# A third expert routed through the slots, with the FFN's second half unrolled

## The chip, the cores and the metric

The kernel runs on one core of one Trainium2 chip. The core's engines run at the same time, each through a program of its own, and wait for one another by semaphores: PE (TensorE) multiplies, DVE (VectorE) and ACT (ScalarE) work elementwise, POOL (GpSimd) does too and issues the indirect DMAs, SP issues the other DMAs. The metric is the device time of one execution in microseconds (us), the median of three runs.

## The reference

4096 rows (2 x 2048) of 256 floats pass through an FFN, causal attention and the same FFN again, each added to what came in. The FFN, shortened:

```python
xln = _ln(x, ln1_w, ln1_b)
att_out = jax.nn.sigmoid(xln @ Wr) * (xln @ Wv) @ Wo
rwkv_state = xln @ Ws
x = x + att_out
h = _ln(x, ln2_w, ln2_b)
...
bids = confidences * capital_shares * difficulty + affinity
winners = jnp.argmax(bids, axis=-1)
...
hr = jnp.square(jax.nn.relu(jnp.einsum('nc,ech->enh', flat_h, K_rwkv)))
out_rwkv = jnp.einsum('enh,ehc->enc', hr, V_rwkv)
out_trans = flat_h @ W1 * jax.nn.sigmoid(flat_state @ W2) @ W3
all_out = jnp.concatenate([out_rwkv, out_trans[None]], axis=0)
...
final = jnp.einsum('ne,enc->nc', onehot, all_out) * scale
return x + final.reshape(B, T, C)
```

Each row needs only the winner's output. Experts 0 and 1 (rwkv) have a hidden width of 1024; the third (trans) has three 256x256 products and a gate made of the first normalized rows z (`flat_state @ W2`).

## The kernel before

A product in float32 is three matmuls (`passes`, L409 to L413): both operands are split in a high and a low part, hi·hi, hi·lo and lo·hi. ACT makes the high parts, DVE or POOL the low ones.

**Part A** of an FFN (`ffn_a_*`) goes through 8 groups (NG) of 512 rows, 4 tiles of 128. For a group PE transposes z (`transpose_z`), projects it (`U`: r, v and the state's gate, 36 matmuls of 512 columns), multiplies by Wo (24 of 256), turns the second normalized rows h (`T2`), computes the bids, then `W1` (12 of 512) and `W3` (24 of 256): the third expert is computed for every row. DVE makes the statistics (`row_stats` L921/927, `stats2` L974/978), the low parts (L949, L960), gv (L954), x2 (L967), the residual (L984), the gates and counts of the routing (`gates` L1000 to L1014, `win` L1018 to L1035, `rank` L1041), the third expert's gate (`g2` L1049) and its sum into the rows (`w3` L1058). POOL turns variances into factors (`rs1` L843 to L848, `rs2` L857 to L860), makes g2's low part (L864) and sends each group's rows, 514 floats long, to their places in a table in DRAM (`scatter` L885, 4 indirect DMAs a group; the last two groups by halves, L875). Rows of expert 0 fill the table from one end, rows of expert 1 from the other. Work on group g is spread over the iterations k = g to g+2; `rows` and `posi` have two buffers, so `residual(g)` waits for the scatter of group g-2 (semaphore `scat`).

**Part B** (`ffn_b_*`) takes the table in 17 slots: 16 of 256 rows and a last one of 128. A slot belongs to expert 0 or 1, read from a table of flags; both K and V stand twice in the program, under `If`/`Else`. PE transposes a slot's h (`sT` L1259), multiplies by K in four quarters (48 matmuls), and V (48 matmuls) one slot behind. ACT makes relu (L1367) and the high part (L1375), DVE the square (L1418), POOL the square's low part (`hr_lo`, L1478), DVE the output rows (`orow` L1425/L1427), which POOL sends back by two indirect DMAs (`send` L1485). Slots 3 to 14 are a loop over two slots on each engine. SP loads a slot's h and rest from the table (L1194, L1199; first use L1206). The table is filled with pad rows ahead of it by SP (`fill`, 16 or 17 DMAs of 514 KB, ahead of each FFN's scatters).

Order on the engines is written by hand, in the loops over k at the end of the functions.

## Times and profile before

| | us |
|---|---|
| runs | 1048.12, 1055.21, 1056.48 |
| median | 1055.21 |
| profiled execution | 1054.12 |
| its span (first to last instruction) | 1052.3 |

| stage | from | to | long |
|---|---|---|---|
| FFN 1, part A (from the first projection) | 12.98 | 207.13 | 194.2 |
| FFN 1, part B, then attention | 207.13 | 661.22 | 454.1 |
| FFN 2, part A | 661.22 | 844.41 | 183.2 |
| FFN 2, part B | 844.41 | 1052.3 | 207.9 |

A stage of part B begins with the first matmul by K of slot 0. Busy shares over the span are PE 93%, DVE 65%, ACT 54% and POOL 47%; the granted TensorE clock has a mean of 0.976. A line of the timeline is: start us, duration us, engine, line, operation, what it writes and reads, how many, and in brackets the idle time of the engine ahead of it with what ended it. In the windows "(x208)" counts instructions.

### The profile page before, as it was taken

What the parts mean: (1) busy time and instruction counts of PE and PEld (TensorE: products, weight loads), DVE (VectorE), ACT (ScalarE), POOL (GpSimd) and SP (SyncE); (2) the same over time, 40 slices, a digit from 0 to 9 for tenths busy, and PEclk for the clock granted to TensorE, in tenths of its full rate; (3) what the DMA queues carried; (4) which work ended last, traced back from release to release, by engine and by line L of the source; (5) the groups of instructions that cost most, each with busy time, mean ns of one, the idle gap of its engine ahead of it and who ended that gap; (6) DMA issues with size and microseconds to landing.
All of it is one profiled execution on the core that took longest, in us unless ns stands there. A gap on an engine that the chain in (4) does not pass through costs nothing.

```text
span 1052.3 us, 21504 instructions
## 1 busy us (share of the span) xinstructions
PE 975.9 (93%) x6960; PEld 900.9 (86%) x6961; DVE 687.6 (65%) x1762; ACT 565.1 (54%) x1201; POOL 490.0 (47%) x539
## 2 busy tenths in 40 slices
...
GB/s 285 178 112 61 81 161 126 96 72 62 61 57 60 60 70 35 111 31 44 65 105 110 51 121 160 101 47 95 62 41 81 81 77 78 60 60 60 61 70 32
DMA packets 51237, 88.96 MB, mean 85 GB/s; under 512 B 5806, under 2 KB 43568, under 8 KB 49968
## 3 DMA queue, kind: packets, MB, share of 16 engines
...
q14 instruction: 34, 0.28, 0.1%
HBM read 58.39 MB, written 47.06 MB: 100 GB/s over the span
## 4 chain that ended last, share of the span: by engine, by line
PE 65%; DVE 18%; ACT 5%; issue 4%; POOL 3%; DMA 1%; another core or an unknown queue 0%; DVEq 0%; POOLq 0%; ACTq 0%; SPq 0%
PE banks4to L412 31%; PE bank L412 24%; PE banks4to L1733 3%; DVE out_rows L1058 2%; DVE pT_lo L2023 2%; DVE gT_lo L960 1%; PE bank L1745 1%; PE bank L508 1%; ACT p L1893 1%; PE bank L1259 1%; DVE chunk_max L2013 1%; POOL attn_x L2121 1%; DVE zT_lo L949 1%; PE bank L498 1%; DVE r_gate L954 1%
## 5 line engine op out<-in xcount | busy, mean ns | idle before, releaser
L1418 DVE TENSOR_TENSOR relu_squared<-relu 128x512 f32<-128x512 f32 (+1 forms) x136 | 151.6, 1124 | 108.1 <-ACT relu L1367 48.6
L1478 POOL TENSOR_TENSOR hr_lo<-relu_squared,hr_hi 128x512 fp32r<-128x512 f32 (+1 forms) x136 | 183.8, 1364 | 58.3 <-DVE relu_squared L1418 55.8
L1367 ACT ACTIVATE relu<-bank,slot_k_bias 128x256 f32<-128x256 f32 (+1 forms) x204 | 83.7, 461 | 177.7 <-PE bank L412 164.0
L412 PE MATMUL banks4to<-v_hi,hr_hi 128*128 128x256 f32 x528 | 151.5, 287 | 2.5 <-DVE slot_out L1427 2.5
L412 PE MATMUL banks4to<-v_lo,hr_hi 128*128 128x256 f32 x528 | 148.7, 282 | 0.0
L412 PE MATMUL banks4to<-v_hi,hr_lo 128*128 128x256 f32 x528 | 148.6, 281 | 0.0
L412 PE MATMUL bank<-shT_hi,k_hi 128*128 128x256 f32 (+1 forms) x408 | 118.1, 289 | 11.1 <-DVE shT_lo L1408 5.8
L412 PE MATMUL bank<-shT_hi,k_lo 128*128 128x256 f32 (+1 forms) x408 | 115.9, 284 | 0.0
L412 PE MATMUL bank<-shT_lo,k_hi 128*128 128x256 f32 (+1 forms) x408 | 115.8, 284 | 0.0
L885 POOL DMA_INDIRECT routed_rows<-out_rows,row_index x48 | 48.1, 1002 | 117.0 <-DVE row_index L1041 106.0
L412 PEld LDWEIGHTS banks4to<-v_hi,hr_hi 128*128 128x128 f32 x528 | 99.5, 188 | 2.9 <-issue 2.9
L412 PEld LDWEIGHTS banks4to<-v_hi,hr_lo 128*128 128x128 f32 x528 | 99.6, 189 | 0.0
L412 PEld LDWEIGHTS banks4to<-v_lo,hr_hi 128*128 128x128 f32 x528 | 99.5, 188 | 0.0
L1375 ACT ACTIVATE hr_hi<-relu 128x512 fp32r<-128x512 f32 (+1 forms) x136 | 84.3, 620 | 16.6 <-ACT relu L1367 8.2
L412 PEld LDWEIGHTS bank<-shT_hi,k_hi 128*128 128x128 f32 x408 | 78.2, 192 | 14.7 <-issue 14.5
L412 PEld LDWEIGHTS bank<-shT_hi,k_lo 128*128 128x128 f32 x408 | 78.3, 192 | 0.0
L412 PEld LDWEIGHTS bank<-shT_lo,k_hi 128*128 128x128 f32 x408 | 78.2, 192 | 0.0
L1893 ACT ACTIVATE p<-banks4to,minus_row_max 128x512 f32<-128x512 f32 (+2 forms) x80 | 49.8, 628 | 35.6 <-DVE minus_row_max L2016 27.8
L1902 ACT CAST pT_hi<-bank 128x512 fp32r<-128x512 f32 (+1 forms) x72 | 39.2, 565 | 41.4 <-PE bank L1745 40.8
L2023 DVE TENSOR_TENSOR pT_lo<-bank,pT_hi 128x512 fp32r<-128x512 f32 (+1 forms) x72 | 47.0, 658 | 19.4 <-ACT pT_hi L1902 18.9
L1485 POOL DMA_INDIRECT x_after_ffn<-slot_out,token_index x33 | 34.3, 1040 | 52.9 <-DVE slot_out L1427 45.5
L1485 POOL DMA_INDIRECT out_x<-slot_out,token_index x33 | 32.6, 989 | 53.7 <-DVE slot_out L1427 46.3
...
## 6 DMA issues: line engine op xcount, KB each, us to landing
...
```

The costliest lines, as they stand in the source:

```text
L412: mm = pe.matmul(outv, w(pw), m(pm), start=(n_first and k == 0), stop=(n_last and k == 2))
L885: pool.indirect_dma_start(routed, bass.IndirectOffsetOnAxis(b.posi[g % 2][:, t:t + 1].bitcast(U32), 0), b.rows[g % 2][:, t, :], None).then ...
L1058: last = dve.scalar_tensor_tensor(rows[:, t, RES], b.bank(6 + t // 2)[:, (t % 2) * C:(t % 2 + 1) * C], b.gt[p][:, t:t + 1], rows[:, t, RES ...
L1367: last = act.activation(b.r[q % 2][:, h % 2, 0:width(j)], b.bank(1 + q)[:, (h % 2) * SLOT:(h % 2) * SLOT + width(j)], ACT.Relu, bias=b.kbs ...
L1375: act.activation(b.hr[p][0][:, 2 * q:2 * q + 2, 0:width(j)], b.r[q % 2][:, :, 0:width(j)], ACT.Square).then_inc(f["hrhi"], 1)
L1418: dve.tensor_tensor(b.sq[q % 2][:, :, 0:width(j)], r, r, ALU.mult).then_inc(f["sq"], 1)
L1478: pool.tensor_tensor(b.hr[p][1][:, 2 * q:2 * q + 2, 0:n], b.sq[q % 2][:, :, 0:n], b.hr[p][0][:, 2 * q:2 * q + 2, 0:n].bitcast(F32), ALU.su ...
L1485: pool.indirect_dma_start(dst, bass.IndirectOffsetOnAxis(b.idx[p][:, t:t + 1].bitcast(U32), 0), b.o[p][:, t, :], None, bounds_check=N - 1, ...
L1733: mm = pe.matmul(out[:, at:at + n], b.kq[pw][:, q, 0, t * P:(t + 1) * P], part, start=(k == 0 and i == 0 and not last), stop=(k == 2), ski ...
L1893: act.activation(b.p[s % 2][t][:, c * KEYS:c * KEYS + w], bank(("S", s, t, c))[:, 0:w], ACT.Exp, bias=b.nbias[:, s % 2, t:t + 1], accum_ou ...
L1902: act.copy(b.pT[m % 2][0][:, 0:w], b.bank(m % 2)[:, 0:w]).then_inc(a["pthi"], 1)
L2023: dve.tensor_tensor(b.pT[m % 2][1][:, 0:w], b.bank(m % 2)[:, 0:w], b.pT[m % 2][0][:, 0:w].bitcast(F32), ALU.subtract).then_inc(a["ptlo"], 1)
```

## The change

Rows of all three experts are routed. The table has three regions of 33 tiles and a pad tile; a row has 770 floats, since it carries z too. Pad rows are written only behind the end of each region (`pads`, 3 indirect DMAs); `fill` is gone. In part A, the state's gate, W1 and W3 are gone from the dense work, with DVE's g2 and w3, POOL's g2 low part and ACT's sig_s and g2_hi; POOL copies z to the rows (`rowz`). The third expert's first products are brought to K's form: for it, a slot's first half is h by W1 and its second half z by the product of Ws and W2, gated by DVE (`gated`), and its W3 stands behind the V of the others. A slot's K of the first half is still chosen by `If`/`Else`; that of the second half is loaded for each slot from DRAM by POOL (`k_in`, 2 DMAs of 512 KB, software queue) in `b.kx`, and V is addressed by a register. There are 18 slots, 16 pairs and 2 singles, unrolled. The first six (EARLY_SLOTS) are made of rows of the first four groups (`early_slots`, in iteration 5 of part A), the others by `late_slots`; the routing of groups 6 and 7 now runs between the first slots of part B.

The core of the diff, on DVE (part A's loop), POOL and PE:

```diff
-ROW = 2 * C + 2
+REGION = N // P + 1
+PAD_TILE = EXPERTS * REGION
+ROWS = (PAD_TILE + 1) * P
+IDX, RES, GATE, Z1 = C, slice(C + 1, 2 * C + 1), 2 * C + 1, 2 * C + 2
+ROW = 3 * C + 2
...
     for k in range(NG):
+        if k:
+            r.residual(k - 1)
+        gv(k, 0)
+        if k >= 2:
+            r.bid_sum(k - 2)
+            r.gates(k - 2)
+        gv(k, 1)
...
+        g_lo(k)
+        if k >= 2:
+            r.win(k - 2)
+            r.rank(k - 2)
+        if k + 1 < NG:
+            z_lo(k + 1)
+        if k:
+            r.h_lo(k - 1)
...
+        if k + 2 < NG:
+            row_stats(dve, b, f, n, k + 2)
+        x2(k)
+        stats2(k)
...
+    def rowz(g):
...
+        if g >= 2:
+            pool.wait_ge(f["scat"][g % 2], 16 * GT * (g // 2))
+        for t in range(GT):
+            last = pool.tensor_scalar(b.rows[g % 2][:, t, Z1:ROW], b.x[g % X_BUFS][:, t], w[:, 4, t:t + 1], w[:, 6, t:t + 1],
+                                      ALU.mult, ALU.add)
...
     for k in range(NG):
-        if 0 <= k - 1:
-            rs2(k - 1)
-        if 0 <= k - 2:
-            lo(k - 2, 0, b.sg[k % 2], b.g2T, f["g2hi"], f["g2lo"])
-            lo(k - 2, 1, b.sg[k % 2], b.g2T, f["g2hi"], f["g2lo"])
+        if k:
+            rowz(k - 1)
         if k + 2 < NG:
             rs1(k + 2)
-        if k == NG - 1:
+        if k == NG - 2:
             pool.drain()
-        if 0 <= k - 2:
+        if k >= 2:
             scatter(k - 2)
+        rs2(k)
...
+    def k_in(j):
...
+        e = pool.value_load(b.slots[0:1, 3, j:j + 1], min_val=0, max_val=EXPERTS - 1)
+        if j >= 2:
+            pool.wait_ge(f["Ks"], 4 * (j - 1))
+        for p in range(2):
+            pool.dma_start(b.kx[j % 2][p][:].rearrange("p c n -> p (c n)"), b.firsts[bass.ds(e * P, P), p]
+                           ).then_inc(f["k_in"][j % 2], 16)
...
+    for j in range(3, NSLOT):
+        for n in range(4):
+            hrlo(j, n)
+        pool.drain()
+        if j + 2 < NSLOT:
+            k_in(j + 2)
+        send(j - 1)
...
+        row = pe.value_load(b.slots[0:1, 2, j:j + 1], min_val=0, max_val=CC + HC)
+        for t in range(tiles_of(j)):
+            for n, h in enumerate((4, 5, 6, 7, 2, 3, 0, 1)):
+                mm = passes(pe, b.bank(0)[:, t * C:(t + 1) * C], lambda p: b.hr[j % 2][p][:, h, t * P:(t + 1) * P],
+                            lambda p: b.V[p][:, bass.ds(row + h, 1)], n == 0, n == HC - 1)
```

POOL's program before, around its scatters of part A; the line numbers in these rows are those of each kernel's own file, a name behind "waits" is the semaphore (`f_st1`: the statistics of the next group's rows, by DVE's row_stats; `f_posr`: the rows' places, by DVE's rank):

```order
L864 TENSOR_TENSOR g2T_lo<-s_gate_62,g2T_hi 128x512 [waits f_g2hi] x2
L843 TENSOR_SCALAR rsqrt_work<-mean_var 128x4 [waits f_z,f_y,f_st1]
L844 TENSOR_SCALAR rsqrt_work<-mean_var 128x4
L845 TENSOR_SCALAR rsqrt_work<-mean_var 128x4
L846 TENSOR_TENSOR rsqrt_work<-rsqrt_work,minus_half 128x8 [waits f_plink]
L848 TENSOR_TENSOR rsqrt_work<-rsqrt_work 128x4 [waits f_plink]
L848 TENSOR_TENSOR rsqrt_work<-rsqrt_work 128x4
L885 DMA routed_rows<-out_rows_64,row_index 4224x514 [waits f_posr,f_rdone,f0_pad]
L885 DMA routed_rows<-out_rows_64,row_index 4224x514 x3
```

The same place in the changed kernel:

```order
L1485 TENSOR_SCALAR out_rows_71<-x_rows_58,rsqrt_work 128x256 x4
L1457 TENSOR_SCALAR rsqrt_work<-mean_var 128x4 [waits f_z,f_y,f_st1]
L1458 TENSOR_SCALAR rsqrt_work<-mean_var 128x4
L1459 TENSOR_SCALAR rsqrt_work<-mean_var 128x4
L1460 TENSOR_TENSOR rsqrt_work<-rsqrt_work,minus_half 128x8 [waits f_plink]
L1462 TENSOR_TENSOR rsqrt_work<-rsqrt_work 128x4 [waits f_plink]
L1462 TENSOR_TENSOR rsqrt_work<-rsqrt_work 128x4
L1495 DMA routed_rows<-out_rows_70,row_index 12800x770 [waits f_rowz,f_posr,f_res,f_z2]
L1495 DMA routed_rows<-out_rows_70,row_index 12800x770 x3
L1471 TENSOR_SCALAR rsqrt_work<-mean_var 128x4 [waits f_z2,f_st2]
```

The place of the scatter behind rs1 is the same; rowz (L1485) stands where the low parts of g2 stood, and rs2 has moved behind the scatter.

DVE's program before, from the residual of iteration 3 (group 2) to the statistics of group 5, in two pieces. First the residual, which waits for the scatter of group 0 (`f0_scattered0`), and what follows it:

```order
L984 SCALAR_TENSOR_TENSOR out_rows_64<-y_rows_59,x_rows_51 128x4x256 [waits f0_scattered0]
L1041 TENSOR_TENSOR row_index<-gate_work,banks4to 128x4 [waits f_pref]
L949 TENSOR_TENSOR hT_lo<-bank,hT_hi 128x512 [waits f_hhi] x2
L967 TENSOR_TENSOR y_rows_60<-banks4to,y_rows_60 128x512 [waits f_Wo,f_y]
L967 TENSOR_TENSOR y_rows_60<-banks4to,y_rows_60 128x512 [waits f_Wo]
```

Then, four rows of `stats2` later, the end of iteration 3 and the start of the next (L921/L927 are row_stats; their end sets `f_st1`, for which POOL's rs1 waits):

```order
L1049 SCALAR_TENSOR_TENSOR s_gate_62<-bank,bias_cols,s_gate_62 128x512 [waits f_W]
L1049 SCALAR_TENSOR_TENSOR s_gate_62<-banks4to,bias_cols,s_gate_62 128x512 [waits f_W]
L990 COPY bid_rows<-banks4to 128x32 [waits f_bidT]
L991 TENSOR_TENSOR bid_rows<-banks4to,bid_rows 128x32 [waits f_link]
L921 BN_STATS bn_parts<-x_rows_51 128x6 [waits f_x_in2,f_st1]
L921 BN_STATS bn_parts<-x_rows_51 128x6 x3
L927 BN_AGGR mean_var<-bn_parts 128x2 [waits f_rs1,f_link]
L927 BN_AGGR mean_var<-bn_parts 128x2 x3
L954 SCALAR_TENSOR_TENSOR r_gate<-bank,bias_cols,r_gate 128x512 [waits f_U,f_sigr]
```

The changed kernel, at the end of iteration 4 and the start of iteration 5:

```order
L1076 TENSOR_TENSOR hT_lo<-bank,hT_hi 128x512 [waits f_hhi] x2
L1045 BN_STATS bn_parts<-x_rows_59 128x6 [waits f_x_in2,f_st1]
L1045 BN_STATS bn_parts<-x_rows_59 128x6 x3
L1051 BN_AGGR mean_var<-bn_parts 128x2 [waits f_rs1,f_link]
L1051 BN_AGGR mean_var<-bn_parts 128x2 x3
L1274 TENSOR_TENSOR y_rows_67<-banks4to,y_rows_67 128x512 [waits f_Wo,f_y]
L1274 TENSOR_TENSOR y_rows_67<-banks4to,y_rows_67 128x512 [waits f_Wo]
L1281 BN_STATS bn_parts<-y_rows_67 128x6 [waits f_x2,f_rs2]
L1281 BN_STATS bn_parts<-y_rows_67 128x6 x3
L1285 BN_AGGR mean_var<-bn_parts 128x2 [waits f_link]
L1285 BN_AGGR mean_var<-bn_parts 128x2 x3
L1082 SCALAR_TENSOR_TENSOR out_rows_70<-y_rows_67,x_rows_57 128x4x256 [waits f0_scattered0]
```

The statistics of the next group (L1045/1051) have moved from the head of an iteration to its end, and the residual (L1082) from its end to the head of the next one, so that x2 and stats2 stand between the two.

## Rows read from the trace of the kernel before

**Rows 1.** Windows: part B of FFN 1, part A of FFN 2; busy us by engine.

```profile
300.00:325.00 25.00, 24.64 (x208) 24.45 (x207) 13.40 (x20) 12.71 (x29) 15.86 (x13) 1.00 0.22 63
...
700.00:725.00 25.00, 24.67 (x154) 21.67 (x154) 21.89 (x77) 17.54 (x34) 10.90 (x16) 1.00 0.18 64
```

**Rows 2.** Timeline of PE: the first matmuls of the four stages.

```profile
12.98 0.77 PE L412 MATMUL bank<-zT_hi,w_hi 128*128 128x512 f32 x1 [0.75 <-DVE zT_lo L949]
...
207.13 0.38 PE L412 MATMUL bank<-shT_hi,k_hi 128*128 128x256 f32 x1 [1.17 <-DVE shT_lo L1408]
...
661.22 0.47 PE L412 MATMUL bank<-zT_hi,w_hi 128*128 128x512 f32 x1 [0.47 <-DVE zT_lo L935]
661.53 0.39 PE L412 MATMUL bank<-zT_hi,w_lo 128*128 128x512 f32 x1
661.76 0.39 PE L412 MATMUL bank<-zT_lo,w_hi 128*128 128x512 f32 x1
...
844.41 0.38 PE L412 MATMUL bank<-shT_hi,k_hi 128*128 128x256 f32 x1 [1.09 <-DVE shT_lo L1408]
```

**Rows 3.** Timeline of DVE in part A of FFN 2, one group.

```profile
733.87 0.75 DVE L1049 SCALAR_TENSOR_TENSOR s_gate<-banks4to,bias_cols,s_gate 128x512 f32<-128x512 f32 x1 [0.49 <-PE banks4to L412]
...
734.86 1.40 DVE L921 BATCH_NORM_STATS2 bn_parts<-x_rows 128x6 f32<-128x256 f32 x4
736.29 0.38 DVE L927 BATCH_NORM_AGGREGATE mean_var<-bn_parts 128x2 f32<-128x6 f32 x4
...
743.72 1.65 DVE L1058 SCALAR_TENSOR_TENSOR out_rows<-banks4to,trans_gate,out_rows 128x256 f32<-128x256 f32 x4
...
746.49 1.22 DVE L984 SCALAR_TENSOR_TENSOR out_rows<-y_rows,x_rows 128x1024 f32<-128x1024 f32 x1
...
754.39 0.75 DVE L1049 SCALAR_TENSOR_TENSOR s_gate<-banks4to,bias_cols,s_gate 128x512 f32<-128x512 f32 x1 [0.47 <-PE banks4to L412]
```

**Rows 4.** Timeline of POOL in the same stretch.

```profile
737.48 0.19 POOL L843 TENSOR_SCALAR rsqrt_work<-mean_var 128x4 f32<-128x4 f32 x1
...
740.07 0.35 POOL L848 TENSOR_TENSOR rsqrt_work<-rsqrt_work 128x4 f32<-128x4 f32 x2
748.56 1.10 POOL L885 DMA_INDIRECT routed_rows<-out_rows,row_index  x1 [8.14 <-DVE row_index L1041]
...
752.51 0.96 POOL L885 DMA_INDIRECT routed_rows<-out_rows,row_index  x1 [0.30 <-issue]
```

**Rows 5.** Timeline of POOL and SP: the last scatter ahead of slot 0's load.

```profile
831.02 0.96 POOL L875 DMA_INDIRECT routed_rows<-out_rows,half_row_index  x1 [0.30 <-issue]
...
833.82 0.99 SPq L1206 DMA_DIRECT2D slot_z<-routed_rows  x2
```

**Rows 6.** Groups of instructions by form, POOL in attention.

```profile
L2121 POOL TENSOR_SCALAR attn_x<-attn_x,mean_var,rsqrt_work 128x256 f32<-128x256 f32 x28 | 34.2, 1231 | 1.5
```

**Rows 7.** Timeline of DVE, then of POOL, in one slot of part B.

```profile
349.82 1.66 DVE L1418 TENSOR_TENSOR relu_squared<-relu 128x512 f32<-128x512 f32 x1 [1.31 <-POOL hr_lo L1478]
...
356.82 0.69 DVE L1418 TENSOR_TENSOR relu_squared<-relu 128x512 f32<-128x512 f32 x1 [0.99 <-ACT relu L1367]
...
347.85 3.08 POOL L1478 TENSOR_TENSOR hr_lo<-relu_squared,hr_hi 128x512 fp32r<-128x512 f32 x2 [0.73 <-DVE relu_squared L1418]
...
356.11 0.99 POOL L1485 DMA_INDIRECT x_after_ffn<-slot_out,token_index  x1 [3.15 <-DVE slot_out L1427]
```

**Rows 8.** Timeline of PE at the end of part A of FFN 2.

```profile
825.87 0.18 PE L535 MATMUL banks4to<-expert_bf,tri_sb 128*128 128x4 bf16 x1
825.91 0.17 PE L536 MATMUL banks4to<-expert_bf,tri_sb 128*128 128x4 bf16 x1
...
837.11 0.58 PE L412 MATMUL banks4to<-w_hi,g2T_hi 128*128 128x256 f32 x1 [9.49 <-DVE g2T_lo L1171]
837.49 0.41 PE L412 MATMUL banks4to<-w_hi,g2T_lo 128*128 128x256 f32 x1
...
842.72 0.60 PE L1259 MATMUL banks4to<-ident_sb,slot_z 128*128 128x128 f32 x4
```

More of the change, by code:

```diff
@@ L148, in build_kernel @@
+        b.sg = at("state_gate", 23056, [2, SLOT])
+        b.o = [at(f"slot_out{i}", 18960 + 512 * i, [ST, C]) for i in range(2)]
+        b.srow = [sb(f"slot_row{i}", [P, ST, Z1 - C]) for i in range(2)]
         b.ax = [at(f"attn_x{i}", 512 * i, [ST, C]) for i in range(AX_BUFS)]
@@ new lines, in routing_vector, with ffn_a_vector, z_lo @@
+    r.link, r.h_lo, r.residual, r.bid_sum, r.gates, r.win, r.rank = link, h_lo, residual, bid_sum, gates, win, rank
+    r.early_slots, r.late_slots = early_slots, late_slots
+    return r
+def ffn_a_vector(dve, b, f, s, n):
+    r = routing_vector(dve, b, f, n)
+    def z_lo(g):
+        for c in range(CC):
+            dve.wait_ge(f["zhi"], 2 * g + 1 + c)
+            dve.tensor_tensor(b.zT[g % 2][1][:, c], b.bank(c), b.zT[g % 2][0][:, c].bitcast(F32), ALU.subtract
+                              ).then_inc(f["zlo"], 1)
@@ new lines, in ffn_b_gpsimd @@
+    pool.wait_ge(f["early"], 1)
+    if s:
+        for one in s.stored:
+            pool.wait_ge(one, 32)
+    k_in(0)
+    k_in(1)
+    tail.rowz(last)
+    for n in range(4):
+        hrlo(0, n)
+    tail.scatter(last - 1)
+    k_in(2)
+    for n in range(4):
+        hrlo(1, n)
+    pool.drain()
+    k_in(3)
+    send(0)
+    hrlo(2, 0)
+    hrlo(2, 1)
+    tail.scatter(last)
+    hrlo(2, 2)
+    hrlo(2, 3)
+    pool.drain()
+    k_in(4)
+    send(1)
+    tail.pads()
+    for j in range(3, NSLOT):
+        for n in range(4):
+            hrlo(j, n)
+        pool.drain()
+        if j + 2 < NSLOT:
+            k_in(j + 2)
+        send(j - 1)
@@ L1634, in attention_sync @@
                 sp.sem_clear(one)
+    pad_tile(sp, f, pad, routed)
     ahead = QB
```

1820 lines of the change are left out of this document (943 added, 877 removed).

## The prediction, made before the changed kernel had run

> **What bounds the kernel now.** I read the windows first, since the two halves of the FFN have different limits. In part B, 208 matmuls and transposes start in 25 us and PE is busy for 24.64 of them [rows 1]: a slot has 48 + 48 matmuls and 4 transposes, so 100 x 25 / 208 = 12.02 us, 0.12 each. PE bounds it; POOL is busy 15.86 of 25. In part A PE looks as full (24.67) but starts only 154 instructions, and DVE is busy for 21.89 of 25. The period of a group is 754.39 - 733.87 = 20.52 us [rows 3], and a 512-column matmul takes 661.76 - 661.53 = 0.23 [rows 2]; 48 of these and 48 of 256 columns are 11.0 + 5.8, and with transposes, bids and prefix I put some 3 more: 19.8 of 20.5. DVE has 21.89 x 20.52 / 25 = 18.0 of 20.5. So PE and DVE both stand near the bound there, and to relieve PE alone would give 2 us a group. The stages are then: FFN 1 part A ends at 207.13, FFN 2 part A is 844.41 - 661.22 = 183.2, and the last part B 1052.3 - 844.41 = 207.9 [rows 2].
>
> **Part A: what goes.** PE loses 24 matmuls of 512 and 24 of 256 a group (8.4 us) and keeps 11.5. DVE loses two g2 (0.65 each, start to start) and w3's four (1.65) [rows 3]; the gates grow by some small linked operations of about 0.2, which I let cancel what the overlap of durations hides: 18.0 - 1.3 - 1.65 and a little gives 15.2 us. PE's 11.5 is then far off, DVE bounds, and I let DVE wait 2.85 a group as it does about now (20.5 - 18.0 = 2.5, and the gates, now directly behind gv, wait for ACT): 18.05 a group.
>
> **Part A: the new wait.** The order on POOL is rs1 of the next group, then the four scatters; that has not changed, but what rs1 waits for has. Today row_stats stands at the head of a DVE iteration and the residual 10 us behind; the scatters wait for row_index (8.14 idle on POOL) [rows 4] and have nearly an iteration to land before the next residual. In the changed order row_stats ends, then only x2 and stats2 follow, then the residual of the next iteration, which overwrites the buffer that the scatter of the group before last reads. From the end of row_stats to the residual's start the chain is rs1, 740.07 + 0.35 - 737.48 = 2.94, with a hand-off 3.1; the scatters, 752.51 + 0.96 - 748.56 = 4.91 [rows 4], with the gap 5.0; and the landing, 833.82 - 831.98 = 1.84 [rows 5], say 1.9. That is 10.1 us; DVE has two x2 and statistics of 1.40 + 0.38 [rows 3] in it, 2.95. It stalls for 7.1, and since this stall also takes in 1.0 of the waits above, a period is 24.2, more than now. It holds for iterations 3 to 6 (the first two scatters have free buffers, and in iteration 6 there is no rs1 ahead of the scatter): 4 x 6.15 = 24.6 a FFN. Behind the residual stand gv, g_lo and z_lo, for which PE and ACT wait.
>
> Eight iterations of 18.05 are 144.4; iterations 0 and 1 lack the routing (about 4.2 each) and some 6 us of iteration 7 lie behind slot 0's start: 129.9. With 24.6 it is 154.5.
>
> **Part A: rowz.** Four tensor_scalars of 1.23 [rows 6] a group are 4.9 us of POOL; it has the time (10.9 of 25 busy [rows 1]), so they cost nothing by themselves. But DVE's square took 1.66 while POOL's hr_lo ran and 0.69 without [rows 7]; the same could befall whatever stands beside rowz, the residual (1.22 [rows 3]) first. I put 5 us for the stage, bounds 0 and 20 (8 x 2.5). In the Trainium skill, "GPSIMD Engine Reference", section 8 (Key points) says that GpSimd shares its SBUF interfaces with VectorE, with contention for DVE instructions in a two-port mode or with two SBUF inputs. By that rule residual and squares suffer, statistics and products with a PSUM input don't, and the sum would have 3 rather than 5; rows 7 agree for the square.
>
> FFN 2 part A: 159.5 for 183.2, **-23.7**. FFN 1 part A has on top: the wait for setup_slots and DVE's splits of the new K halves, 20.5 by count of instructions, and 1.5 more contention through v_lo on POOL: 12.98 + 154.5 + 20.5 + 6.5 = 194.5 for 207.1, **-12.6**.
>
> **Part B: a slot.** Four more transposes: the four of 842.72 took PE some 0.43 [rows 8]; 12.02 + 0.43 + 0.1 = 12.55. V's matmuls come in triples with two register instructions between, 32 or more a slot. PE can start two small matmuls 0.04 apart (825.87, 825.91 [rows 8]) and needs 0.12 for one of 256 columns, so I hide them: nothing, at most 0.14 x 16 triples = 2.3 a slot. Before the trace shows no such row. POOL gets k_in, two DMAs; by its indirect ones (0.96 + 0.30 [rows 5]) 2.5 us, bounds 0.5 and 5. It stands where POOL idled 3.15 for slot_out (356.11 [rows 7]), so it is nearly covered; for what is left, and for `gated` and the second slo on DVE, I put 0.25 a slot. A pair is 12.8.
>
> **Part B: the whole.** Slots 0 to 3 would take 50; in between lie the routing of groups 6 and 7, whose scatters stand on POOL between the low parts, and late_slots, some 50 linked operations on DVE (12 us) ahead of slot 3's squares. By walking the order I come to 65. Twelve pairs at 12.8 are 153.6; two singles (8.2 each, of which one is new) with the tail 27.3. Sum 245.9 for 207.9: **+38**, for both FFNs **+76**. Attention keeps its order; the pad fills that vanish beside it are SP's and hidden.
>
> Profiled: 1054.1 - 23.7 - 12.6 + 76 = 1093.8; the median shown, 1055.2, lies 1.1 above the profiled execution: **1095 us**. Its own range is 1072 to 1118 (the bounds of rowz and k_in, 60 to 70 for the first slots).
>
> **Rivals.** (1) POOL doesn't delay DVE in part A: the stall of 6.15 and the contention are absent, because scatters land while PE and ACT are late anyway. For it speaks that 8.14 of slack stand there now [rows 4]; against it that the slack is by the row_index, not by rs1. It gives 1095 - 49.2 - 11.5 = 1034, faster. It decides once 50 of these 61 us are gone, that is a stall under about 1 us a period. (2) Slots bound by POOL: 5.2 of hr_lo (4 x 1.3, and 3.08 for two when DVE works beside it [rows 7]), 2.5 k_in, 2.5 send, and the idle of 3.15 and 0.7 that remains because each piece waits for DVE: 14.0. Against it: k_in lies in the idle. 24 pairs x 1.2 = 29: 1124. (3) PE slows: after 9.49 us idle the granted clock was at its lower level (1.2 of 2.4 GHz), a 256-column matmul took 0.41 for 0.28 [rows 8]; in part A PE will idle half of every period, and if gv, Wo and the transposes run so on the path, 2.3 us a period are 37; the same or more if V's triples aren't hidden. Around 1135, up to 1165. The Trainium skill, "TensorE: Matmul & The Clock Gate", Part 1, says that an idle array falls to half rate; rows 8 agree, and by the rule every period of part A would begin so. (4) The stall is half and part B starts better: within 1% of 1055. A change that does nothing is no case: the counts of slots don't hang on the data.
>
> **Chances.** Forecast 0.47, (1) 0.19, (2) 0.16, (3) 0.10, (4) 0.08. A difference under 1% can't be told from none here. Faster comes from (1), slower from the forecast, (2) and (3): 0.19, 0.08, 0.73. The range takes in (1) and (2) and the near end of (3): 1032 to 1135.
>
> **What would show it.** The stall: DVE's residual in iterations 3 to 6 with 6 to 7 us idle ahead of it, ended by a POOL scatter, and periods of 24 us; absent, (1) holds and PE's first K of FFN 2 comes 130 us after its first projection, not about 160. rowz: residual or g_lo at twice its duration. Part B: windows of 25 us with some 203 matmuls and transposes (104 each 12.8); if POOL is busy over 90% there, (2) holds; a triple of V longer than 0.36 or a clock under 0.9 in part A, (3). The first slots: K of slot 4 some 65 us after that of slot 0; less, and late_slots are hidden. The prediction is wrong as a whole if part A saves over 50 an FFN, or if part B's pair takes 12.1 or over 14.

## The result: 1189 us, 13% slower, and the profile after

| | before | changed |
|---|---|---|
| median of the runs, us | 1053.44 | 1189.37 |
| lowest to highest | 1048.12 to 1056.48 | 1182.58 to 1192.29 |
| profiled execution, span | 1052.3 | 1180.9 |

The ratio is 1.1297, with a 95% interval of 1.126 to 1.1335. The forecast was 1095 in a range of 1032 to 1135: the direction was right, the size was not; the loss is 136 us where 40 were forecast. (The median before is now of four runs, the fourth 1051.67.)

The page of the changed kernel, its first part (busy us, share of the span, instructions) and the granted clock and DMA traffic in 40 slices:

```profile
span 1180.9 us, 20296 instructions
...
PE 916.3 (78%) x6490; PEld 850.7 (72%) x6490; DVE 711.3 (60%) x1870; ACT 589.3 (50%) x1279; POOL 537.0 (45%) x656
...
PEclk8877777898999999989999999987779897999999
```

PE starts fewer matmuls than before (6490 for 6960) and is busy for 78% of a longer span where it was 93%. The clock's digits, 9 in nearly all slices before, are 7 in most of both parts A (slices 3 to 7 and 28 to 30). The first matmuls of the stages, as in [rows 2], from the timeline of PE:

```profile
13.83 0.77 PE L419 MATMUL bank<-zT_hi,w_hi 128*128 128x512 f32 x1
```
```profile
219.07 0.38 PE L419 MATMUL bank<-slot_zT_hi,k_hi 128*128 128x256 f32 x1 [2.11 <-DVE slot_zT_lo L1360]
```
```profile
734.49 0.48 PE L419 MATMUL bank<-zT_hi,w_hi 128*128 128x512 f32 x1 [0.47 <-DVE zT_lo L1059]
```
```profile
907.23 0.38 PE L419 MATMUL bank<-slot_zT_hi,k_hi 128*128 128x256 f32 x1 [2.10 <-DVE slot_zT_lo L1360]
```

| stage | before | forecast | changed | miss |
|---|---|---|---|---|
| FFN 1, until slot 0 | 207.1 | 194.5 | 219.1 | +24.6 |
| FFN 1 part B and attention | 454.1 | 492.1 | 515.4 | +23.3 |
| FFN 2 part A | 183.2 | 159.5 | 172.7 | +13.2 |
| FFN 2 part B | 207.9 | 245.9 | 273.7 | +27.8 |

Two windows of 25 us as in [rows 1], part B and part A (busy us by engine in the order PE, PEld, DVE, ACT, POOL, with the instructions; granted clock; DMA share; GB/s):

```profile
425.00:450.00 25.00, 22.62 (x187) 22.20 (x187) 13.23 (x20) 12.46 (x28) 15.40 (x15) 1.00 0.51 152
825.00:850.00 25.00, 14.10 (x72) 12.52 (x72) 13.20 (x48) 10.42 (x21) 11.55 (x18) 0.77 0.17 66
```

In part B only 187 matmuls and transposes start where 208 did: a slot of 104 takes 13.9 us by this count, and 13.87 from slot to slot in the mean of slots 4 to 15 of FFN 2. No engine is full: PE is busy 22.6, DVE 13, ACT 12, POOL 15 of 25. In part A, too, PE is busy 14 and DVE 13 of 25, at a mean clock of 0.77. So in both parts a chain through several engines seems to set the time, and no engine's sum of work; the experiments test it.

**Part A's chain.** DVE, then POOL, at the end of iteration 4 and the start of 5 of FFN 2 (timeline: start, duration, engine, line; in brackets the idle time ahead):

```profile
807.41 0.38 DVE L1051 BATCH_NORM_AGGREGATE mean_var<-bn_parts 128x2 f32<-128x6 f32 x4
...
810.66 0.38 DVE L1285 BATCH_NORM_AGGREGATE mean_var<-bn_parts 128x2 f32<-128x6 f32 x4
818.48 1.23 DVE L1082 SCALAR_TENSOR_TENSOR out_rows<-y_rows,x_rows 128x1024 f32<-128x1024 f32 x1 [7.44 <-DMA routed_rows<-out_rows,row_index]
```
```profile
807.88 0.20 POOL L1457 TENSOR_SCALAR rsqrt_work<-mean_var 128x4 f32<-128x4 f32 x1 [11.98 <-DVE mean_var L1051]
...
811.27 1.09 POOL L1495 DMA_INDIRECT routed_rows<-out_rows,row_index  x1 [0.46 <-issue]
...
815.21 0.96 POOL L1495 DMA_INDIRECT routed_rows<-out_rows,row_index  x1 [0.30 <-issue]
...
818.55 3.24 POOL L1485 TENSOR_SCALAR out_rows<-x_rows,rsqrt_work 128x256 f32<-128x256 f32 x4 [0.44 <-DMA routed_rows<-out_rows,row_index]
```

It is the forecast's stall, step by step. The statistics end at 807.8, rs1 runs from 807.88, the four scatters from 811.27 to 816.17, and the residual (L1082) begins when the last has landed, at 818.48, after 7.44 us of idle. The list of waits (in total, times, longest) has all eight, with the normalizing of h on ACT that writes the same buffer, and the wait that matters in part B:

```profile
DVE relu_squared L1369 <- POOL hr_lo L1541: 160.2, 34, 5.4
...
DVE out_rows L1082 <- DMA routed_rows<-out_rows,row_index: 54.2, 8, 9.4
...
ACT out_rows L813 <- DMA routed_rows<-out_rows,row_index: 45.1, 8, 7.4
POOL kx_hi L1559 <- issue: 39.7, 23, 3.3
```

**Part B's chain.** One slot in the middle of FFN 2, on POOL, then on DVE, then PE's start of the next slot:

```profile
1061.01 2.56 POOL L1541 TENSOR_TENSOR hr_lo<-relu_squared,hr_hi 128x512 fp32r<-128x512 f32 x2
1064.28 1.27 POOL L1541 TENSOR_TENSOR hr_lo<-relu_squared,hr_hi 128x512 fp32r<-128x512 f32 x1 [0.70 <-DVE relu_squared L1369]
1068.08 1.29 POOL L1541 TENSOR_TENSOR hr_lo<-relu_squared,hr_hi 128x512 fp32r<-128x512 f32 x1 [2.53 <-ACT hr_hi L990]
1071.03 0.59 POOL L1559 DMA_DIRECT2D kx_hi<-first_product_halves  x1 [1.67 <-issue]
1071.64 0.57 POOL L1559 DMA_DIRECT2D kx_lo<-first_product_halves  x1
1072.51 1.04 POOL L1548 DMA_INDIRECT out_x<-slot_out,token_index  x1 [0.30 <-issue]
1073.85 1.01 POOL L1548 DMA_INDIRECT out_x<-slot_out,token_index  x1 [0.30 <-issue]
1074.86 1.32 POOL L1541 TENSOR_TENSOR hr_lo<-relu_squared,hr_hi 128x512 fp32r<-128x512 f32 x1
```
```profile
1062.44 1.70 DVE L1369 TENSOR_TENSOR relu_squared<-relu 128x512 f32<-128x512 f32 x1 [5.07 <-POOL hr_lo L1541]
1064.06 1.28 DVE L1360 TENSOR_TENSOR slot_zT_lo<-banks4to,slot_zT_hi 128x512 fp32r<-128x512 f32 x2
1065.26 0.58 DVE L1379 TENSOR_SCALAR state_gate<-state_gate,slot_relu 128x512 f32<-128x512 f32 x1
...
1066.66 0.69 DVE L1383 TENSOR_TENSOR relu_squared<-relu,state_gate 128x512 f32<-128x512 f32 x1
```
```profile
1065.06 0.38 PE L419 MATMUL bank<-slot_zT_hi,k_hi 128*128 128x256 f32 x1 [1.26 <-DVE slot_zT_lo L1360]
```

From one first low part on POOL (1061.01) to the next (1074.86) it is 13.85. The third square on DVE waits 5.07 us for the first low part (1062.44; it shares the square's buffer), then come the next slot's two low parts of h (slo, L1360), the gated quarter (L1379 to L1383), ACT's high part, the fourth low part on POOL (1068.08, after 2.53 idle), 1.67 without a busy instruction (a drain and the read of the expert's number), k_in (1071.03 and 1071.64), the two sends, and the next slot's first low part. PE waits 1.26 for slo in it.

### The profile page after: what moved, and what is told of

It is laid out like the page before. It is cut to its first block, busy times and chain, and to the rows that moved or that the text cites. A ratio compares the mean times of both kernels' runs of the same rounds, so it can differ in the third digit from the quotient of the medians.

```text
span 1180.9 us, 20296 instructions
## 1 busy us (share of the span) xinstructions
PE 916.3 (78%) x6490; PEld 850.7 (72%) x6490; DVE 711.3 (60%) x1870; ACT 589.3 (50%) x1279; POOL 537.0 (45%) x656
## 4 chain that ended last, share of the span: by engine, by line
DVE 17%; PE 14%; issue 10%; POOL 8%; ACT 5%; POOLq 2%; DMA 2%; DVEq 0%; ACTq 0%; SPq 0%
PE bank L419 6%; PE banks4to L1879 3%; PE banks4to L419 3%; POOL hr_lo L1541 2%; POOL out_x L1548 2%; DVE slot_zT_lo L1360 2%; DVE pT_lo L2169 1%; POOLq L1590 1%; ACT p L2039 1%; PE bank L1891 1%; DVE chunk_max L2159 1%; DMA routed_rows<-out_rows,row_index 1%; POOL attn_x L2267 1%; POOL routed_rows L1495 1%; DVE state_gate L1381 1%
## 5 line engine op out<-in xcount | busy, mean ns | idle before, releaser
L419 PE MATMUL bank<-v_hi,hr_hi 128*128 x544 | 157.2, 289 | 6.8 <-POOL hr_lo L1541 6.8
L419 PE MATMUL bank<-v_lo,hr_hi 128*128 x544 | 154.2, 283 | 0.0
L419 PE MATMUL bank<-v_hi,hr_lo 128*128 x544 | 154.1, 283 | 0.0
L419 PEld LDWEIGHTS bank<-v_hi,hr_hi 128*128 128x128 f32 x544 | 104.4, 192 | 7.5 <-issue 7.5
L419 PEld LDWEIGHTS bank<-v_hi,hr_lo 128*128 128x128 f32 x544 | 104.3, 192 | 0.0
L419 PEld LDWEIGHTS bank<-v_lo,hr_hi 128*128 128x128 f32 x544 | 104.1, 191 | 0.0
L419 PE MATMUL bank<-slot_zT_hi,kx_hi 128*128 128x256 f32 (+1 forms) x288 | 84.8, 294 | 16.9 <-DMA kx_lo<-first_product_halves 9.4
L964 ACT ACTIVATE relu<-bank,slot_k_bias,slot_relu 128x256 f32<-128x256 f32 (+1 forms) x144 | 71.1, 544 | 45.9 <-DVE relu_squared L1369 24.7
L419 PE MATMUL bank<-slot_zT_lo,kx_hi 128*128 128x256 f32 (+1 forms) x288 | 84.1, 292 | 0.0
L419 PE MATMUL bank<-slot_zT_hi,kx_lo 128*128 128x256 f32 (+1 forms) x288 | 84.1, 292 | 0.0
```

The lines of the kernel that those rows point to most:

```text
L419: mm = pe.matmul(outv, w(pw), m(pm), start=(n_first and k == 0), stop=(n_last and k == 2))
L964: last = act.activation(b.r[n % 2][:, h, 0:m], raw, ACT.Relu, bias=b.kb[:, j, at:at + 1], scale=b.fl[:, j:j + 1])
```

## The experiments

All times are medians beside runs of the kernel before on the same chip; the ratio is to these. Changed kernel: 1.1297. A period or a gap is read off the first matmul of a group's projection, or of a slot, in each trace.

### The stall of part A

`e1_scatter_first`, POOL's order:

```diff
-        if k + 2 < NG:
-            rs1(k + 2)
         if k == NG - 2:
             pool.drain()
         if k >= 2:
             scatter(k - 2)
+        if k + 2 < NG:
+            rs1(k + 2)
         rs2(k)
```

> On POOL, part A, the scatters of group k-2 stand ahead of rs1(k+2), not behind it; nothing else differs from the changed kernel. Theory (the residual waits for rs1, then four scatters, then the landing): the row's places are there 6.6 us before rs1 can start (827.3 against 833.7 in the changed kernel), so the idle time of 6.8 us mean (54.2 us, 8 times) ahead of the residual goes, and PE's low clock in those periods with it in part: 1189 - 54 = 1135, and periods of 25 to 27 us in iterations 3 to 6 of FFN 2 fall to 18 to 19.5. Rival (POOL's amount of work or PE's low clock, not the order, makes the periods long): periods stay over 24 and the time over 1175.

Measured: 1144.6 us, ratio 1.0871 (1.0839 to 1.0903): 45 us gained of the 54 expected. The residual of the same place waits for nothing:

```profile
790.45 0.38 DVE L1285 BATCH_NORM_AGGREGATE mean_var<-bn_parts 128x2 f32<-128x6 f32 x4
790.75 1.20 DVE L1082 SCALAR_TENSOR_TENSOR out_rows<-y_rows,x_rows 128x1024 f32<-128x1024 f32 x1
```

Periods of iterations 3 to 6 in FFN 2, 25.2, 26.5, 27.3 and 25.1 in the changed kernel, are 20.7, 20.6, 20.8 and 23.4. So the order made the stall. But 20.6 is no less than the 20.5 of a period before the change, though DVE has only 15.3 us of work in it: the expected 18 to 19.5 was too low.

`e9_stats_at_head` undoes DVE's part instead:

```diff
         if k:
             r.residual(k - 1)
+        if k + 2 < NG:
+            row_stats(dve, b, f, n, k + 2)
         gv(k, 0)
...
-        if k + 2 < NG:
-            row_stats(dve, b, f, n, k + 2)
         x2(k)
```

> The changed kernel with one part of the change undone: DVE makes the statistics of group k+2 (row_stats) near the head of an iteration, as before the change, not behind h_lo; POOL's order stays as changed (rs1, then the scatters). Theory (the stall needs both that rs1 stands ahead of the scatters and that its statistics are late): rs1 is done before the row's places are there, the scatters start by row_index as in the kernel before, the residual waits for nothing, and the time is that of e1_scatter_first, 1145, with periods of 20 to 21 us. Rival (landing of 770-float rows, not the order, makes the residual late): 1175 to 1190, the residual still idles over 4 us.

Measured: 1151.8, ratio 1.0923 (1.0896 to 1.0949), 38 us gained; periods of FFN 2 from iteration 2 on 20.7, 20.7, 20.5, 20.7, 23.4. The wait of the residual (L1082) for the scatters is in the list of waits of neither e1 nor e9. So taking back either half of the pair (late statistics, rs1 ahead of the scatters) takes the stall away, and the longer rows, which both runs keep, don't make it.

`e5_pe_kept_busy` adds to e1, behind the prefix sums:

```diff
             r.prefix(k - 2)
+            pe.wait_ge(f["sigr"], 2 * k + 2)
+            for _ in range(34):
+                pe.matmul(b.bank(4)[:, 0:CC * P], b.Wb[:, 0], b.Wb[:].rearrange("p c n -> p (c n)"), start=True, stop=True)
         if k:
             r.T2(k - 1)
```

> e1_scatter_first with 34 throwaway matmuls of 256 columns on PE between the prefix sums and the transposes of h, in iterations 2 to 7 of part A, where PE idles 4.9 us for DVE's z_lo. Theory (the rest of a period of part A beyond DVE's 15.3 us of work, 20.6 in e1, is in part PE at its lower clock behind that idle time: transposes of 1.94 for 1.04 us, 24 matmuls of Wo at 0.21 for 0.12): the transposes take 1.04, the period falls to 18.5 to 19.5, and the time to 1144 - 10 x 1.5 = 1129. Rival (the clock doesn't matter, since DVE waits for ACT and for the order of z_lo): under 4 us in all.

Measured: 1143.7, ratio 1.0866 (1.0824 to 1.0909), against e1's 1.0871: no difference to be told, where 15 us were expected. PE of e1, then of e5, at the transposes of h, and a window of one period of each:

```profile
802.77 1.94 PE L488 MATMUL bank<-ident_sb,out_rows 128*128 128x128 f32 x8 [4.93 <-DVE zT_lo L1255]
```
```profile
792.71 4.31 PE L626 MATMUL banks4to<-w_bid 128*128 128x256 f32 x34
797.78 1.06 PE L488 MATMUL bank<-ident_sb,out_rows 128*128 128x128 f32 x8 [0.76 <-DVE zT_lo L1258]
```
```profile
789.00:809.50 20.50, 13.98 (x76) 12.38 (x75) 15.31 (x54) 11.37 (x22) 11.23 (x19) 0.83 0.28 102
```
```profile
789.00:809.50 20.50, 17.35 (x115) 15.00 (x114) 15.67 (x57) 11.87 (x25) 11.95 (x21) 1.00 0.27 104
```

The clock went from 0.83 to 1.00 and the transposes from 1.94 to 1.06 us, so the first half of the mechanism is right, and iterations 2 to 5 of FFN 2 got 0.8 to 1.4 us shorter each (19.4 to 20.0). But the edit stands in iteration 7 too, where the transposes of h otherwise follow the prefix sums directly, and there the matmuls stand in PE's way:

```profile
854.93 4.32 PE L626 MATMUL banks4to<-w_bid 128*128 128x256 f32 x34
```

From the start of iteration 7 to slot 0 it is 21.2 us for 19.6 in FFN 2 and 20.9 for 18.1 in FFN 1. So the time of the whole kernel doesn't price the clock, the periods do: five of them (iterations 2 to 6) are 4.4 us shorter together in FFN 2 and 1.7 in FFN 1, some 6 us where rival 3 said 37. Even this is near what two traces of one order differ by: part A of FFN 2 takes 155.9 us in e1 and 150.3 in e6, which has the same part A.

`e8_v_lo_on_dve` moves the nine low parts of V from POOL to DVE:

```diff
+        if s and k in (4, 5):
+            for i in range(0, 5) if k == 4 else range(5, V_ITEMS):
+                raw, _, hi, lo = v_plan(b)[i]
+                dve.wait_ge(s.v_hi, i + 1)
+                dve.tensor_tensor(lo, raw, hi.bitcast(F32), ALU.subtract).then_inc(s.v_lo, 1)
```

> e1_scatter_first with the nine low parts of V (FFN 1, iterations 4 and 5) made by DVE behind stats2, not by POOL. In the changed kernel DVE's small operations beside them took 1.1 to 1.2 us where they take 0.17 elsewhere. Theory (what a POOL operation with two inputs costs DVE is its whole duration, for each small DVE operation that meets it): DVE gets 9 x 0.6 = 5.4 us of work and loses 2 x 4.3 us of such waits, and POOL's rowz and row scatters come earlier: 1144 - 5 = 1139, iterations 4 and 5 of FFN 1 shorter by 2 to 4 us each. Rival (POOL's time is hidden and DVE bounds): 1144 + 5 = 1149.

Measured: 1141.2, ratio 1.0845 (1.0801 to 1.0888); periods of iterations 5 and 6 of FFN 1, 24.5 and 29.4 in e1, are 21.1 and 27.0. The intervals of e1 and e8 overlap, so the evidence is in the two periods: part A of FFN 1 is 5.9 us shorter, and in the five later runs with this edit and four or five known groups (e12 to e16) it is 3.5 to 5 us shorter than in e6. Whether DVE's waits beside POOL's operations do it, or POOL's own queue, whose rowz and scatters come earlier too, this run doesn't separate.

### A slot of part B

`e2_k_in_in_gap`:

```diff
-        for n in range(4):
+        for n in range(3):
             hrlo(j, n)
         pool.drain()
         if j + 2 < NSLOT:
             k_in(j + 2)
+        hrlo(j, 3)
         send(j - 1)
```

> In part B from slot 3 on, POOL's two loads k_in(j+2) stand between the third and the fourth low part of slot j, where POOL idles 2.53 us for ACT's hr_hi, and not behind the fourth. Theory (a slot's 13.87 us is a chain that closes over POOL: low parts, wait for the gated quarter, loads, sends, next low part): 3.1 us of loads fall into 2.5 us of idle, a slot takes 12.6 to 12.9, and the time is 1189 - 26 x 1.1 = 1160. Rival (the chain closes over DVE and ACT, or PE is held by register-addressed matmuls): the slot stays over 13.6 and the time over 1180.

Measured: 1142.9, ratio 1.0864 (1.0834 to 1.0894): 46 us gained, more than expected, since a pair now takes 12.3 us and not 12.6 to 12.9. A window of its part B, and POOL there:

```profile
1000.00:1025.00 25.00, 25.00 (x213) 25.00 (x212) 16.10 (x23) 15.55 (x33) 17.74 (x17) 1.00 0.53 170
```
```profile
1024.61 0.59 POOL L1559 DMA_DIRECT2D kx_hi<-first_product_halves  x1 [1.66 <-issue]
1025.22 0.57 POOL L1559 DMA_DIRECT2D kx_lo<-first_product_halves  x1
1025.80 1.30 POOL L1541 TENSOR_TENSOR hr_lo<-relu_squared,hr_hi 128x512 fp32r<-128x512 f32 x1
```

213 matmuls and transposes start in 25 us, PE is full, and with 1.66 idle and the two loads the fourth low part starts directly behind. The 13.87 - 12.3 = 1.57 us a slot were the place of k_in on POOL; below that PE bounds, so how much more of the chain's 3.1 us is hidden now can't be seen.

`e3_no_k_in_after_slot_4` leaves k_in(5) and later out, so that the later slots use the halves of K that slots 3 and 4 loaded (PE's wait for the loads is changed with it):

```diff
-        if j + 2 < NSLOT:
-            k_in(j + 2)
```

> Leaves out the loads of the second half of K (k_in) from slot 5 on; the slots use what slots 3 and 4 loaded, so the products of those slots are of another expert's weights. Theory of the chain over POOL: 3.2 us of POOL go from each slot, PE bounds, and a slot takes 12.5 to 12.7 us (100 matmul places plus four transposes), the time 1189 - 36 = 1153. Rival (DMA traffic of 150 GB/s or PE's registers make the slot long): with the traffic gone but the chain elsewhere the slot stays over 13.5; were it PE's registers, over 13.5 too.

Measured, one run: 1146.2 us beside 1053.3, and 12.3 us a slot again. So with the loads gone a slot isn't shorter than with them in the gap (170 GB/s in e2's window): the DMA traffic did not make it long, and neither did PE's registers, which both runs keep. V's triples in the changed kernel's trace show the latter too:

```profile
1058.17 0.29 PE L419 MATMUL bank<-v_lo,hr_hi 128*128 x1
1058.30 0.28 PE L419 MATMUL bank<-v_hi,hr_hi 128*128 x1
1058.42 0.28 PE L419 MATMUL bank<-v_hi,hr_lo 128*128 x1
```

A register instruction stands on each side of 1058.17, and the matmuls are 0.12 apart, as before. A slot has 16 such instructions there, two to each of 8 triples, and not the 32 that the prediction feared.

`e6_scatter_and_k_in` has both edits, e1 and e2.

> The edits of e1_scatter_first and e2_k_in_in_gap together. Theory (one lies in part A, the other in part B, and both are the longest chain of their part): the gains of 44.8 and 46.5 us add up, 1189 - 91 = 1098. Rival (they share slack at the seam of the parts): a part of the gain is lost, over 1110.

Measured: 1102.1, ratio 1.0486 (1.0445 to 1.0528): 87 us gained of 91, so the two chains are separate within the intervals. Of the loss of 136 us, 49 to 52 are left.

### The first slots of part B

In the changed kernel and in e6 the gaps from slot to slot at the start of FFN 2's part B are 16.3, 17.8, 14.3, 25.7 and 17.5, 16.2, 17.4, 24.3 us, where 12.3 is a slot. PE ahead of slot 4, with DVE and POOL before it, in the changed kernel:

```profile
981.36 0.58 PE L419 MATMUL bank<-slot_zT_hi,k_hi 128*128 128x256 f32 x1 [12.18 <-DVE slot_zT_lo L1360]
```
```profile
959.32 3.13 DVE L1199 SCALAR_TENSOR_TENSOR table_work_e<-table_work_e 128x3 f32<-128x3 f32 x1
```
```profile
959.91 2.51 POOL L1541 TENSOR_TENSOR hr_lo<-relu_squared,hr_hi 128x512 fp32r<-128x512 f32 x2
...
973.55 1.16 POOL L1501 DMA_INDIRECT routed_rows<-pad_rows,pad_row_index  x1 [4.01 <-DVE slot_numbers L1163]
...
977.27 2.50 POOL L1541 TENSOR_TENSOR hr_lo<-relu_squared,hr_hi 128x512 fp32r<-128x512 f32 x2
```

PE waits 12.18. DVE numbers the late slots from 958.0 to 973.3 in front of slot 3's squares, 15.3 us, of which 3.13 are one 128x3 operation beside two low parts; then the pad scatters (973.55 to 977.26) stand in front of POOL's first low part. They wait for the flag at the end of the numbering, though DVE wrote their index at 958.16 and POOL was idle for the 4.01 us ahead of them; no run lets them go earlier.

`e4_late_slots_in_two` (on the changed kernel):

```diff
-    r.late_slots()
+    piece = r.late_slots()
     for j in range(3, NSLOT):
         for n in range(3):
+            if n == 2 and j in (3, 4):
+                next(piece)
             sq(j, n)
```

> The some 50 small operations that number the late slots are cut in two pieces, which DVE runs between its second and third square of slots 3 and 4, where it idles 4 to 5 us for POOL's low part; the three pad scatters stand between POOL's second and third low part of slot 4. Theory (they cost their own 14 us, since slot 3's squares stand behind them): PE's wait of 12.4 us ahead of K of slot 4 goes, and some 4 to 6 us come back as the pieces are longer than the idle time: 8 us a FFN, 1189 - 16 = 1173. Rival (the slots 3 and 4 wait for something else, such as their rows): under 5 us in all.

Measured: 1187.0, ratio 1.1288 (1.1253 to 1.1323): not to be told from the changed kernel. The gap ahead of slot 4 fell from 25.7 to 17.8, and the next two rose from 15.1 and 12.7 to 18.9 and 20.2; then two slots took 12.3. The second piece was 11 us long, and slot 6's rows, which wait for it, came 3.7 us late. 3.33 of the 11 are one operation beside two low parts (979.68 on POOL):

```profile
978.96 3.33 DVE L1229 TENSOR_SCALAR table_work_slots<-table_sb,table_work 128x13 f32<-128x13 f32 x1
```

`e7_seam` is e6 with the numbering in two pieces (the first where it was, the second in slot 3), pads behind POOL's second low part of slot 3, z_lo(k+1) ahead of `win`, and in part A:

```diff
         if k:
             rowz(k - 1)
+        if k == NG - 1:
+            pool.wait_ge(f["early"], 1)
...
+            load_k(pool, b, f, 0)
+            load_k(pool, b, f, 1)
```

> e6_scatter_and_k_in with three edits more: DVE makes z_lo(k+1) ahead of the winners' rows in part A; POOL issues the loads for slots 0 and 1 in iteration 7 of part A, where it idles 6 us for row_index; the numbering of the late slots is cut in two, the first piece where it was, the second between the second and third square of slot 3, with the pad scatters behind POOL's second low part there. Theory: 1.3 us a period of part A (10 in all), 4.8 us a FFN of PE's wait for kx_lo in slot 0, 5 us a FFN of the 12.4 us ahead of slot 4: 1098 - 10 - 9.6 - 10 = 1068. Rival (the first slots are one chain through the routing of groups 6 and 7, and what one wait loses the next gets back): 1085 to 1098.

Measured: 1099.4, ratio 1.0451 (1.0409 to 1.0492): 3 us of the 30 expected, the rival's range. Part A of FFN 2 got 1.8 us shorter, that of FFN 1 4.4 us longer (189.7 for 185.3 from the first projection); the wait for slot 0's kx went, and the routing's matmuls (idle 5.13 ahead of the prefix sums) and slot 1 took its place: the first five gaps sum to 88.8 us against 89.3.

`e10_six_groups_known` (KNOWN = 6, ten early slots, on e6) and `e11_six_known_v_lo` (with e8's edit):

```diff
-KNOWN = 4
+KNOWN = 6
```

> e6_scatter_and_k_in, with ten early slots drawn from the first six groups in place of six from four, and the numbering of the late slots in three pieces between the second and third squares of slots 3, 4 and 5, the pad scatters in slot 6. Slot 0 then waits for the early numbers (4.5 us of DVE in iteration 7, no longer in 5) and for the scatter of group 5. Theory (DVE is full in the first slots: routing of groups 6 and 7, 14 us of numbering, the slots' own 8 us each; the pieces fall into idle time of some 5 us a slot only from slot 3 on, and run 1 to 3 us over): slot 0 starts 5 us later, the gap ahead of slot 4 falls from 24 to 17 and the next two grow to 14: 3 us lost or gained a FFN, 1095 to 1108. Rival (the numbering itself, not the sum of DVE's work, holds the first slots): 8 us or more gained a FFN, under 1087.

> e10_six_groups_known with V's low parts on DVE, as in e8_v_lo_on_dve. Theory (what e8 gained, 3.4 us, comes from POOL operations beside DVE's small ones in iterations 4 and 5, and adds up): 3 to 5 us under e10. It is the fastest form of the change that these runs point to, and is still slower than the kernel before: over 1080.

Measured: 1123.2 (1.0648, 1.0618 to 1.0679) and 1116.0 (1.0578, 1.0552 to 1.0604). Slot 0 of FFN 2 starts 15 us later in its stage, not 5, as the early numbers, SP's loads by them and slot 0's transposes now follow one another behind iteration 7. Part A of FFN 1 is 13.5 longer. The eight gaps from slot 0 of FFN 2 sum to 124.6, in e6 to 126. e10 missed its expectation, and e11 is 7 below it.

`e12_e6_v_lo` (e6 and e8), `e13_pads_later` and `e14_five_groups_known` ran side by side. e13's edit on POOL and e14's:

```diff
-    tail.pads()
...
+            if j == 3 and n == 2:
+                tail.pads()
             hrlo(j, n)
```

```diff
-KNOWN = 4
+KNOWN = 5
...
+            if n == 2 and j in (3, 4, 5):
+                next(piece)
             sq(j, n)
```

> e6_scatter_and_k_in with V's low parts on DVE (as in e8): the base of the two runs beside it, and the sum of three edits. Theory (independent chains): 1102 - 3.4 = 1098.7. Rival (no sum): 1102.

> e12_e6_v_lo with the three pad scatters between POOL's second and third low part of slot 3 instead of ahead of its first. Theory (the 24 us ahead of K of slot 4 are one chain: 14 us of numbering on DVE, then the pads' 3.7 us on POOL, then the first low part, for which the third square waits): the gap falls by 3 to 4 us a FFN and 6 to 7 us are gained, 1092. Rival (the first slots are held by the sum of DVE's work, and the next gap grows): under 2 us.

> e12_e6_v_lo with eight early slots drawn from the first five groups, early numbers in iteration 6 (not 5, and not 7 as in e10), the late numbering in three pieces between the second and third squares of slots 3, 4 and 5, pads in slot 5. Theory (in e10 slot 0 started late because the early numbers came behind iteration 7; the pieces themselves cost less than the lump): slot 0 starts as in e12, the eight gaps from slot 0 on are those of e10 (124.6 us with 16.8 for the pads) or some 4 us less, against 126 in e12: 1 to 6 us a FFN, 1088 to 1096. Rival (the first slots lose to the routing of groups 6 and 7 whatever the numbering does): within 2 us of e12.

Measured: 1097.1 (1.0373 to 1.0444), 1094.7 (1.0358 to 1.0441) and 1097.8 (1.038 to 1.0451). The three can't be told apart, so the expected 1092 of e13 and the gain of e14 did not come; both times are nearer to the rivals'. In e13 the gap ahead of slot 4 fell from 24.0 to 21.4 and the next rose from 14.1 to 16.2; in e14 slot 0 started in time, the gaps 3 to 6 were 18.1, 16.1, 13.7 and 18.6 (the last with the pads) for 24.0, 14.1, 12.3, 12.3.

`e15_numbering_half_twice` and `e16_24_ops_in_steady_slots`, on e12:

```diff
+        for again in range(2):
           dve.tensor_tensor(tiles, ...
```

```diff
             if n == 2 and j in (8, 9):
+                for _ in range(24):
+                    r.link(dve.tensor_scalar(b.t1[:, 11:12], b.t1[:, 4:5], 1.0, None, ALU.mult))
             sq(j, n)
```

> e12_e6_v_lo with the first 23 operations of the late numbering done twice (the same inputs give the same values), in the same place ahead of slot 3's squares: about 4 us more on DVE in each FFN. Theory (the numbering's place is on the chain of the first slots for its whole length, and what its removal to other places gave back was lost to those places): 4 us a FFN, 1097 + 8 = 1105, and the gap ahead of slot 4 is 28. Rival (the first slots are held by the routing of groups 6 and 7 and the numbering is partly hidden): under 3 us.

> e12_e6_v_lo with 24 small linked operations (0.2 us each, 4.8 us) on DVE between the second and third square of slots 8 and 9, where it waits 3 to 4 us for POOL's low part. Theory (a slot at 12.3 us is bounded by PE, and DVE has some 5 us to spare, but only in this place): 0 to 1 us a slot, 1097 to 1101. Rival (in the place where e14's pieces stood there is no room): 4 us a slot or more, 1097 + 16.

Measured: 1103.3 (1.0518, 1.049 to 1.0545) and 1096.8 (1.0446, 1.0425 to 1.0466). PE ahead of slot 4 in e12, then in e15:

```profile
917.25 0.58 PE L419 MATMUL bank<-slot_zT_hi,k_hi 128*128 128x256 f32 x1 [11.49 <-DVE slot_zT_lo L1365]
```
```profile
923.68 0.58 PE L419 MATMUL bank<-slot_zT_hi,k_hi 128*128 128x256 f32 x1 [15.56 <-DVE slot_zT_lo L1366]
```

With 4 us more numbering in each FFN the wait grew by 4.07 and the gap from 24.0 to 28.0 in both FFNs; the time is 6.6 us above e16's, which ran beside it on the same chip. So the numbering has no slack behind it: what is added to it comes out in full. That all of it could be gained by taking it away isn't shown. In e16 the gaps of slots 8 and 9 stay at 12.3 with 4.8 us of small operations in each, so there they cost nothing. What stays open is why the numbering could not be moved to slots 3 to 5 with profit: there the slots are not yet at 12.3, and each piece and the pads brought 2 to 6 us with them, of which e4's operation of 3.33 is a part; which of DVE's and POOL's waits carries the rest of the first slots' excess (the first five gaps take some 26 us a FFN over 12.3 a slot) was not separated from the routing of groups 6 and 7.

No version ran faster than the kernel before: the lowest, e13, is at 1.04. By stages e12 shows why: part A takes 195.4 for 207.1 and 155.0 for 183.2, 40 us saved, but part B with attention takes 493.3 for 454.1 and the last part B 252.1 for 207.9, 83 us more. The largest piece of the loss that was read is the first slots: the first four gaps of the last part B take 73.6 us for 54.8 before. The rest, with the added slot in it, was not divided further.

## Why the prediction was wrong

**What bounds each part (right as far as it went).** DVE's and PE's sums were near the traced ones: DVE has 15.3 us of work in a period of e1 (15.2 said).

**The new wait (right).** The chain was told as it came: 10.1 us said from the end of the statistics to the residual, 818.48 - 807.79 = 10.7 traced; 7.1 of idle said, 6.8 the mean (54.2 us in 8). e1 and e9 show it by both of its ends. Rival 1, which denied it, is refuted.

**The rest of a period (too small).** The term by which DVE waits 2.85 a period, "about as it does now", was mis-sized: without the stall a period is 20.6, so 5.3 are waits (the transposes of h stand on PE behind z_lo, and DVE's hT_lo waits 1.94 for them). In the changed kernel periods are 25 to 27 for 24.2. In part A of FFN 2 the miss of 13 us is 4 x 1.8 in iterations 3 to 6, 4 in iteration 2 and 7 in iteration 7 (19.1 us to slot 0 for 12.05), less the 5 of rowz, which were added and did not show.

**FFN 1's part A (too small, 24.6).** The same 13, and 11 more. "1.5 more contention through v_lo" was said, and with these operations off POOL the stage is 5.9 us shorter (e8 against e1); the other 7 or so were not traced. DVE and POOL in iteration 5 of FFN 1:

```profile
154.09 1.19 DVE L1097 TENSOR_TENSOR expert_bids<-expert_bids,conf_rows 128x12 f32<-128x12 f32 x1
```
```profile
149.34 7.14 POOL L1508 TENSOR_TENSOR v_lo<-raw_v_lo,v_hi 128x512 fp32r<-128x512 f32 x5
```

A 128x12 operation takes 1.19 us beside v_lo, and 0.17 in FFN 2 (821.27). rowz was shorter than thought (2.2 to 3.2 us for four, not 4.9), and its sign, a residual of twice its duration, did not come: the residual took 1.23 us beside it for 1.22 before, and it was rowz that was longer there (3.24 for 2.2). What contention there was fell on POOL and not on the residual.

**A slot of part B (the failed step, 13 us a FFN).** This is where the mechanism was wrong and not only a size. "It stands where POOL idled 3.15 for slot_out, so it is nearly covered" took the idle time's place from the kernel before. The gated quarter has moved POOL's idle time ahead of the fourth low part; behind it k_in is bare: 1.67 idle, 1.18 for the two loads and 0.30 to the send are 3.15 in a chain that closes over the next slot. 0.25 was said, 1.57 measured by e2. Rival 2 had the slot right (14.0 for 13.87) and its sum nearly too: low parts, k_in and sends, and POOL's waits of 3.85 (3.23 traced, 0.70 and 2.53) one behind the other. Against it stood "k_in lies in the idle", which was the error. Only its sign did not come, POOL busy over 90%, for waits are in its chain and POOL is busy 15 of 25 us. The four transposes cost 0.2 and not 0.5: a pair takes 12.33 in e2 for 12.11 before (six gaps in the middle of FFN 2). The V by register was hidden, as said.

**The first slots (too small, 9 to 10 us a FFN) and the end (6).** 65 us were said for slots 0 to 3, 74.1 and 75.5 came. The numbering was priced at 12 and took 15.3, and the pads (3.7) behind it were not in the walk; e15 shows that the numbering has no slack behind it. The last slots, still in the chain of 13.7, and the tail took 33.0 for 27.3.

**Rival 3 (clock).** The clock fell as it said, to 0.77 in part A, but raised it gave back some 6 us in all by the periods of e5, for 37 said. In the Trainium skill, "TensorE: Matmul & The Clock Gate", Part 1, an idle array falls to half rate; the trace agrees (eight transposes took 1.94 us behind 4.93 idle, 1.06 behind 0.76). But what DVE waits for here is in small part PE's speed.

**The sum.** The misses are 24.6 + 23.3 + 13.2 + 27.8 = 88.9; the rest to 94 is that the profiled execution is the lowest of its runs. The range failed because the bounds of parts A and B were not added: it took one rival at a time, and here the slots' chain, the longer periods and the first slots came together.
